# Where the index rows of the copied tiles come from: made by VectorE in the preparation and kept in DRAM, in place of a word-by-word read of the source list

## The reference, cut to what matters

```python
# layer 0: x -> x1
h   = concat([x[src], edge_attr], axis=1) @ W1 + b1      # 400000 x 64
msg = silu(batchnorm(h))                                 # mean and variance over all edges
agg = segment_sum(msg, dst) / max(count(dst), 1)
x1  = layernorm(x + silu(batchnorm(concat([x, agg], axis=1) @ W2 + b2)))
# layer 1: x1 -> out
msg = relu(x1[src] + edge_attr)
agg = segment_sum(msg, dst)
out = layernorm(x1 + relu(((1 + eps) * x1 + agg) @ W.T + b))
```

## Time and profile before

| | |
|---|---|
| median of 3 runs | 8551.34 us (8548.04 to 8551.66) |
| profiled execution, its own time | 8550.71 us |
| its span, first to last instruction | 8548.9 us |
| busy: POOL | 5791.3 us (68%) |
| busy: PE | 5401.2 us (63%) |
| busy: DVE, ACT | 3025.1 us (35%), 2802.2 us (33%) |
| transfers of under 512 B | 560,180 of 821,774 |

### The profile page before, as it was taken

One profiled execution on the slowest core, in us unless ns is written; L12 is line 12 of the kernel. 1 busy time (PEld: TensorE's weight loads), 2 busy tenths in 40 slices (PEclk: granted clock), 3 DMA queues, 4 the chain that ended last, 5 costly groups with the idle time before them and its releaser, 6 DMA issues. The chain is left out here.

```text
span 8548.9 us, 118413 instructions
## 1 busy us (share of the span) xinstructions
PE 5401.2 (63%) x23204; PEld 3178.1 (37%) x23204; DVE 3025.1 (35%) x20741; ACT 2802.2 (33%) x17905; POOL 5791.3 (68%) x6026
## 2 busy tenths in 40 slices
PE   4555555555555555553798566766766666666666
PEld 2222222222222222221797333433433333333334
DVE  3222222222222222222686444444444444444444
ACT  0111111111111111110576555555555555555553
POOL 7777777777777777774000477777777777777774
PEclk7555556555555555555898655555555555555555
DMA  3333333333333333332575122222222222222221
GB/s 100 79 77 78 78 78 78 78 78 78 78 78 78 78 78 78 78 78 42 156 198 157 46 55 55 55 55 54 55 55 55 55 55 55 56 55 55 56 54 41
DMA packets 821774, 630.75 MB, mean 74 GB/s; under 512 B 560180, under 2 KB 643307, under 8 KB 820629
## 3 DMA queue, kind: packets, MB, share of 16 engines
q1 hardware_dynamic: 582330, 323.43, 14.7%
q0 software_dynamic: 192480, 200.41, 12.2%
q10 hardware_dynamic: 46450, 102.55, 3.9%
HBM read 516.99 MB, written 108.90 MB: 73 GB/s over the span
## 5 line engine op out<-in xcount | busy, mean ns | idle before, releaser
L390 POOL DMA_INDIRECT Z<-in_x_dram,src_idx x3125 | 2988.7, 956 | 971.3 <-issue 951.1
L1220 POOL DMA_INDIRECT X<-x_scratch,src_idx x2877 | 2765.4, 961 | 902.2 <-issue 851.4
L1292 ACT ACTIVATE rows_by_act<-table 64x4 uint8 x15872 | 1567.8, 189 | 828.1 <-issue 825.0
L424 PE MATMUL PS<-ident,Z 128*128 128x128 f32 x3125 | 745.0, 397 | 1688.0 <-DMA Z<-in_x_dram,src_idx 1681.0
L475 ACT ACTIVATE ZT<-PS 128x640 f32<-128x640 f32 x625 | 439.5, 703 | 3504.9 <-PE PS L424 3504.9
L1329 DVE COPY rows_by_dve<-table 64x4 uint8 x15872 | 1219.6, 193 | 960.2 <-issue 960.0
L435 PE MATMUL PS<-ZT,W_sb 128*64 128x320 f32 x2500 | 1462.7, 740 | 0.0
L1236 PE MATMUL PS<-X,ident 128*128 128x320 f32 x1002 | 685.0, 785 | 1153.2 <-DMA X<-x_scratch,src_idx 1153.2
L541 DVE BATCH_NORM_STATS2 stats<-PS 128x320 f32 (+1 forms) x624 | 279.5, 490 | 3040.2 <-remote 3018.4
L424 PEld LDWEIGHTS PS<-ident,Z 128*128 128x128 f32 x3125 | 524.9, 201 | 2020.2 <-issue 1740.1
L1231 PE MATMUL PS<-E,ident 128*128 128x320 f32 x1250 | 872.9, 801 | 1.7 <-ACT table L1296 1.7
(11 more groups left out here) (144 smaller groups left out, 3512.2 us busy)
## 6 DMA issues: line engine op xcount, KB each, us to landing
Z<-in_edge_attr_dram SPq DMA_DIRECT2D x625, 160.0 KB, 3.3
E<-in_edge_attr_dram SPq DMA_DIRECT2D x625, 160.0 KB, 2.2
h_scratch<-h_ring ACTq DMA_DIRECT2D x312, 320.0 KB
hT<-h_scratch SPq DMA_DIRECT2D x312, 320.0 KB
Z<-in_x_dram,src_idx POOLq DMA_INDIRECT x3125, 2.5
X<-x_scratch,src_idx POOLq DMA_INDIRECT x2877, 2.5
x_nodes<-in_x_dram SPq DMA_DIRECT2D x1, 3125.0 KB
x_ring<-in_x_dram SPq DMA_DIRECT2D x25, 125.0 KB
```

What stands on the lines that cost most here:

```text
L390: nc.gpsimd.indirect_dma_start(out=Z[:, r, j, 0:D], out_offset=None, in_=x, in_offset=bass.IndirectOffsetOnAxis(ap=src_idx[:, n:n + 1], ax ...
L424: last = nc.tensor.transpose(banks(2 * (s % 2), 2, P, EG)[:, j * P:(j + 1) * P], Z[:, r, j, :], ident[:, :])
L1220: nc.gpsimd.indirect_dma_start(out=X[:, r, j, :], out_offset=None, in_=x1_dram, in_offset=bass.IndirectOffsetOnAxis(ap=src_idx[:, n:n + 1] ...
L1292: return act.activation(to, of, ACT.Copy)
```

## The change

The word-by-word transfers at the end of the first gather stage go away, and with them the DVE operation that made byte addresses in the second gather stage. In their place DVE makes the byte addresses of the two columns in the preparation, from `src_rows`, which there stands in SBUF as float (`at_rows`, two operations of 125 x 128). SP stores them to DRAM as its last transfer of the preparation (125 rows of 1 KB) and loads them back into `copied_at`, laid out as `copied_src` was, in two transfers of 4 x 31 pieces of 512 B, between its tenth and its eleventh edge load of the first gather stage. ACT and DVE wait in the second gather stage for the loads, not for the DVE operation.

```diff
-        copied_src = sb(ctx, "copied_src", [2 * PERIODS, BODIES, P], int32)
-        src_copied = ctx.enter_context(nc.semaphore("src_copied"))
+        copied_at = sb(ctx, "copied_at", [2 * PERIODS, BODIES, P], int32)
+        copied_at_stored = ctx.enter_context(nc.semaphore("copied_at_stored"))
+        copied_at_loaded = ctx.enter_context(nc.semaphore("copied_at_loaded"))
+        copied_at_dram = nc.dram_tensor("copied_at_scratch", (SB, 2, P), int32, kind="Internal").ap()
...
                         sp.dma_start(x_nodes[:, :], x_v.rearrange("p t c -> p (t c)")).then_inc(s_x, 16)
+                        sp.wait_ge(at_made, 2)
+                        sp.dma_start(copied_at_dram, at_rows[:, :, :]).then_inc(copied_at_stored, 16)
...
                             nc.vector.tensor_copy(part.bitcast(fp32), part).then_inc(src_float, 1)
+                        dve.wait_ge(src_float, S)
+                        for row, j in enumerate((BY_DVE, BY_ACT)):
+                            nc.vector.tensor_scalar(at_rows[:, row, :], index_tiles(src_rows)[:, COPIED_SLOT % S, j, :],
+                                                    float(WORD), float(TABLE_AT), ALU.mult, ALU.add).then_inc(at_made, 1)
                         dve.wait_ge(s_const, 1)
...
                         for s in range(slots):
+                            if isinstance(k, int) and k == 0 and s == RING:
+                                sp.wait_ge(copied_at_stored, 16)
+                                for row in range(2):
+                                    sp.dma_start(copied_at[row * PERIODS:(row + 1) * PERIODS, :, :],
+                                                 copied_at_dram[1:, row, :].rearrange("(k t) p -> t k p", t=PERIODS)
+                                                 ).then_inc(copied_at_loaded, 16)
                             wait_at(sp, rows_done, k, BODY, s + 1 - RING)
...
                     sp.wait_ge(s_x, 16)
-                    for j, row in ((BY_DVE, 0), (BY_ACT, 1)):
-                        for T in range(PERIODS):
-                            of = src.rearrange("(g p j) -> j g p", p=P, j=TG)[j, COPIED[T]::BODY, :]
-                            sp.dma_start(copied_src[PERIODS * row + T:PERIODS * row + T + 1, :, :], of.unsqueeze(0),
-                                         allow_slow_non_contiguous=True).then_inc(src_copied, 16)
...
-                    act.wait_ge(nodes_ready, 1)
+                    act.wait_ge(copied_at_loaded, 32)
...
-                    dve.wait_ge(src_copied, 16 * 2 * PERIODS)
-                    nc.vector.tensor_scalar(copied_src[:, :, :], copied_src[:, :, :], float(WORD), float(TABLE_AT), ALU.mult,
-                                            ALU.add).then_inc(nodes_ready, 1)
-                    dve.wait_ge(nodes_ready, 1)
+                    dve.wait_ge(copied_at_loaded, 32)
```

More of the change, by code:

```diff
@@ L244, in gnn_kernel @@
             ones_row = sb(here, "ones_row", [1, P])
+            at_rows = sb(here, "at_rows", [SB, 2, P], int32)
+            at_made = sem("at_made")
             ones_col = sb(here, "ones_col", [P, 1])
@@ L1151, in gnn_kernel @@
             hot = sb(here, "hot_c", [P, RING, TG, WIN])
-            nodes_ready = sem("nodes_ready")
             rows_dve = sb(here, "rows_by_dve", [D, 2, P])
@@ L1181, in copy_rows @@
                 _, nodes = nc.values_load_multi_w_load_instructions(
-                    copied_src[row:row + 1, ds(at(k, 1, 0), 1), step * STEP:(step + 1) * STEP].rearrange("o a n -> o (a n)"),
+                    copied_at[row:row + 1, ds(at(k, 1, 0), 1), step * STEP:(step + 1) * STEP].rearrange("o a n -> o (a n)"),
                     [kind], min_val=TABLE_AT, max_val=TABLE_AT + WORD * (NODES - 1), skip_runtime_bounds_check_because="src holds numbers of nodes")
```

## The result

The changed kernel takes 8437.7 us (median of 4 runs, 8432.01 to 8441.9), the kernel before 8549.69 us beside it (8547.06 to 8551.66). The ratio is 0.9869, 95% interval 0.9852 to 0.9886: about 112 us faster. The forecast was 8444 us in a range of 8437 to 8455, so the median lies 0.7 us above the lower end. The profiled execution of the changed kernel took 8441.9 us.

The account below looks back on a forecast made before the run. SP's queue of eight word copies was taken to hold 113.38 us between the last statistics operation and the first silu. Profiled 8550.71 less 107.1 gives 8443.6, plus 0.6 to the median: 8444 us, range 8437 to 8455.

Parts of the forecast that it names:

- the copies don't hold the stage: End of first gather stage: copies landed under cover, something else makes the gap, time stays 8551 us; rival, chance 0.03.
- the first silu 107.1 us earlier: Start of message stage: without the copies, ACT's first silu comes at 4006.2 us against 4113.28.
- the landing of the first load: Start of message stage: first hT load on an idle queue lands in 4.3 us, bounds 3.9 to 8.
- the barrier, taken as 1.51 us: End of first gather stage: from the last arrival at the barrier to SP's first hT issue, 1.51 us.
- the later start by the store: Preparation: SP's store delays the whole first gather stage by 0.5 us, bounds 0.3 to 1.2.
- POOL's stretch from first to last gather: First gather stage: POOL paces it, 3,125 gathers of 1.26 us each; the stage only shifts with POOL's first gather.
- I cost this at nothing: Second gather stage: removing DVE's 2.31 us address operation gains nothing, at most ACT's wait of 3.4 us.
- The added work: Preparation and first gather stage: two DVE operations up to 0.9 us, covered; store 0.5 us; two small loads, covered.
- some of the cover at the start fails: Edge loads behind the store or a slower first hT burst cost 10 to 40 us: 8454 to 8484; chance 0.06.
- the hold falls on the third transfer: Start, behind x_nodes: the third transfer was held 24.22 us; with the store ahead, the second edge load may be.
- The store is held: Preparation: store held 24.2 us behind x_nodes, and the barrier with it, giving 8468 us; rival, chance 0.05.
- The pause buys the clock: Message stage: PE's full clock comes from the 115 us pause; without it up to 8944 us; rival, chance 0.03.

Follow-up runs that it names:

- the covered copies: Kernel before, its eight word copies issued one behind each of the last eight full bodies of edge loads: 8445.2 us, ratio 0.9875.
- four and six: Changed kernel with four, or six, of the eight word copies put back behind the last edge loads, and the address operation: 8467.93 us and 8519.56 us.
- the three stores: Changed kernel with the store of the preparation made three times, two of them into spare rows of DRAM: 8457.87 us (one run).
- the `hT` loads from elsewhere: Changed kernel with the first five hT loads of the message stage taken from the edge rows in DRAM: 8448.23 us (one run).
- the window in PSUM: Changed kernel with the hot_c comparison reading its window numbers from a PSUM bank, segment sums on two banks, not four: 8408.03 us, ratio 0.9825.

## Why the prediction was right, step by step

**How close it was.** The forecast of 8444.2 us is 6.5 us above the median of 8437.7. Against the profiled execution, 8441.9, the forecast for it of 8443.6 is 1.7 too high; the median before was 0.6 above its profiled execution, and the median after is 4.2 below. Two of the four runs, 8432.01 and 8433.74, lie under the range, so that the median fell just inside it is partly luck. The mechanism was right: the terms below show it.

**The path was the one described.** SP's queue held the barrier and then the first `hT` load. Taken away (the change), put under cover (the covered copies) or put back in part (four and six), the first silu moves as a queue of slow transfers says. Rival *the copies don't hold the stage* is refuted by all three.

**The terms.** The prediction put the first silu 107.1 us earlier; it came 4113.28 - 4001.06 = 112.2 earlier. The 5.1 us between are:

- the landing of the first load, taken as 4.3 us, was 2.85: 1.4. This was the worst sized term, and the edge loads of the earlier trace rows, in a burst, were a poor model for it. But it varies from 2.68 to 5.20 between executions, so no single number was to be had.
- the barrier, taken as 1.51 us, was 1.25: 0.3. The 1.25 is the same in nearly every profile of a kernel without the copies at the end.
- the later start by the store, taken as 0.5 us, was 29.74 - 29.52 = 0.22: 0.3.
- POOL's stretch from first to last gather was 3937.0 us against 3939.5, and the tail behind it 30.25 against 30.91: 3.2. The prediction had both unchanged. That is scatter: the changed kernel's three profiles give 3937.0, 3936.5 and 3940.3.

From the silu to the end the profiled execution gave 3.4 us back (8440.1 - 4001.06 against 8548.9 - 4113.28), nearly all of it in the second gather stage (3643.5 us of gathers against 3640.5, where repeats of the changed kernel gave 3634.6 and 3636.7). So the profiled execution is 108.8 us shorter, and the medians 112.0 apart.

**The step that failed** is "I cost this at nothing", for the address operation. Its cover was judged by who waits for it, which are ACT and PE behind POOL. It also acts on POOL itself, which nobody covers: 1.6 us for the one gather beside it, in the kernel before too (its longest gather of that stage takes 2.56 us). That DVE operations can stretch a neighbour's gather stood in the 3450 ns maximum of the earlier trace rows, which the prediction passed over. The kernel with the operation put back was 12 us slower than the changed one beside it, and only 1.6 of these are shown. In both its profiles the median gather of the second stage took 947 ns and in all three profiled executions of the changed kernel 944 or 945; over the 6,002 gathers of both stages 2 to 3 ns would be 12 to 18 us. But other kernels without the operation (the three stores, the `hT` loads from elsewhere, the window in PSUM) have 947 too, so it isn't the operation's doing by this evidence, and the other 10 us stay open.

**The added work** behaved nearly as costed. The second edge load was held 19.45 us as the prediction allowed, and PE started tile 0 only 0.8 us later than before; POOL never waited for PE in the stage, so *some of the cover at the start fails* did not occur. One of the two small loads took 0.85 us, over the 0.7 that was given as the most, under the same cover. That the hold falls on the third transfer was read rightly before and held in the changed kernel, but it is no rule, as the three stores showed. *The store is held* did not occur (0.33 us).

**The pause buys the clock** is refuted. The granted clock was 0.50 at the start of work in either kernel and reached 1.00 within 20 us, with the pause and without; and from the first silu to the first load of the next stage (`x_ring`, at 4638.86 us before and 4526.54 after) the profiles show 525.6 us before and 525.5 after.

## What to carry to other kernels

Where a stage ends in a barrier, look at what each queue still holds, its DMA issue time included: a transfer of 3,968 single words costs its queue some 25 us here, and everything behind it waits. Moving such transfers to a place with cover came within 7 us of removing them here, a difference that the runs can't tell from none, so try the move first. And where GpSimd's gathers set the pace, look at which DVE operations run beside the longer ones: one input moved from SBUF to PSUM was worth 39 us here, about a third of what the whole change brought.

## What the hardware showed beyond that

DVE operations with both inputs in SBUF, and the address operation from SBUF to SBUF, stretch a gather that GpSimd issues beside them: 0.94 us became 1.02 on average beside `hot_c` (272 of 645 over 1.0), and 2.56 beside the 8 x 3968 address operation; the comparison with one input in PSUM did nothing of the kind (0 of 622). The Trainium skill, SBUF — State Buffer (section on who interferes with whom), says that a DVE instruction with two SBUF inputs contends with a GpSimd instruction that reads SBUF, and so does one in certain fast modes, while one with a single SBUF input outside these modes doesn't. The runs agree for two inputs, with gathers that read their indices in SBUF, and for one input in the reduction above, which stretched none. That the address operation ran in such a mode no run here shows. In the first gather stage of the changed kernel 130 of the 517 gathers beside `hot_a` take over 1.0 us, and the 517 together some 29 us more than at the usual pace. There every PSUM bank is written by TensorE, and a form without the second SBUF input wasn't tried.

The usual gather itself differs between the profiled executions, with medians of 944 to 947 ns in the second stage that hold for the whole of it. Whether one and the same program can have both wasn't seen: the changed kernel had 944 or 945 in its three profiles. So this is not what sets those three apart. Two of them differ by 8.9 us in the second gather stage (3643.5 and 3634.6), and just that much lies in the stretched gathers: those over 1.0 us take 46.6 us more than the usual in the one and 37.7 in the other. How the comparisons happen to fall on the gathers is thus a part of this kernel's spread, and it limits what a comparison of single profiles can show.
